# Graph attention: query and key products moved by one round, into the rounds that also aggregate

## The reference, cut to what matters

```python
for l in range(L):                                    # L = 2, H = 8, DH = 64
    q = ((x @ Wq[l].T + bq[l]) * scaling).reshape(n, H, DH)
    k = (x @ Wk[l].T).reshape(n, H, DH)
    v = (x @ Wv[l].T).reshape(n, H, DH)
    scores = jnp.einsum('ehd,ehd->eh', q[tgt], k[srcidx])
    m = jax.ops.segment_max(scores, tgt, num_segments=n)
    p = jnp.exp(scores - m[tgt])
    s = jax.ops.segment_sum(p, tgt, num_segments=n)
    w = p / (s[tgt] + 1e-16)
    agg = jax.ops.segment_sum(w[:, :, None] * v[srcidx], tgt, num_segments=n)
    attn = agg.reshape(n, D) @ Wo[l].T + bo[l]
    x = _batchnorm(x + attn, g1[l], beta1[l])
    ff = jax.nn.relu(x @ W1[l].T + b1[l]) @ W2[l].T + b2[l]
    x = _batchnorm(x + ff, g2[l], beta2[l])
```

## Time and profile before

| | |
|---|---|
| median of 3 runs | 1181.24 us |
| the profiled execution | 1181.42 us |
| its span in the trace | 1179.7 us |
| TensorE busy | 1076.4 us, 91% |
| VectorE busy | 642.7 us, 54% |
| ScalarE busy | 410.5 us, 35% |
| mean granted TensorE clock | 0.973 |
| attention of layer 0, rounds | about 505 to 738 us |
| attention of layer 1, rounds | about 835 to 1067 us |

### The profile page before, as it was taken

How to read it: one execution, slowest core, us unless ns; L and a number is a source line. 1 busy time by engine, 2 the same in 40 slices (tenths; PEclk the granted TensorE clock), 3 DMA queues, 4 the chain that set the end, 5 groups by cost and what they waited for, 6 DMA issues and landing times.

```text
span 1179.7 us, 14861 instructions
## 1 busy us (share of the span) xinstructions
PE 1076.4 (91%) x5638; PEld 693.6 (59%) x5638; DVE 642.7 (54%) x1162; ACT 410.5 (35%) x560; POOL 177.5 (15%) x119
## 2 busy tenths in 40 slices
PE   6999999899878999989999999989899999999914
PEld 2726446687657867656666666434566666664413
DVE  5685666446684145246565664541455555654495
ACT  2401112354323122045454554110455555551004
POOL 2000000997144420000000000000000000003000
PEclk9999999899989999999999999999999999999967
DMA  8001000002000310200000020110000000100002
GB/s 313 36 0 36 36 18 1 1 1 72 1 1 1 108 36 1 72 1 1 1 1 1 1 73 1 35 37 36 1 1 1 1 1 1 37 1 19 1 0 72
DMA packets 17659, 31.08 MB, mean 26 GB/s; under 512 B 3708, under 2 KB 4924, under 8 KB 17342
## 3 DMA queue, kind: packets, MB, share of 16 engines
q1 hardware_dynamic: 14270, 28.08, 6.8%
q10 hardware_dynamic: 3328, 2.15, 0.6%
HBM read 28.12 MB, written 2.10 MB: 26 GB/s over the span
## 4 chain that ended last, share of the span: by engine, by line
PE 81%; DVE 10%; ACT 3%; issue 2%; POOL 2%; DMA 1%; DVEq 0%; SPq 0%; ACTq 0%; POOLq 0%
PE slots L1516 71%; PE slots L1583 11%; DVE PT L1343 1%; DVE KS L1333 1%; DMA W<-in_wkT 1%; POOL KR L583 1%; ACT KS L873 1%; POOL MASK L584 1%; DVE rstd L1207 0%; DVE SM L1397 0%; DVE X L1409 0%; DVE XT L1291 0%; DVE P0L L1172 0%; DVE st L945 0%; DVE st L1414 0%
## 5 line engine op out<-in xcount | busy, mean ns | idle before, releaser
L1516 PE MATMUL slots<-XT,W 128*128 128x512 f32 x320 | 143.0, 599 | 0.0
L1516 PE MATMUL slots<-KS,QS 64*128 64x512 f32 x768 | 108.6, 416 | 18.3 <-DVE KS L1333 9.9
L1516 PE MATMUL slots<-PT,XN 128*64 128x256 f32 x1024 | 117.6, 382 | 0.0
L971 DVE COPY PT<-slots 128x1024 f32<-128x1024 f32 x64 | 78.2, 1222 | 71.1 <-PE slots L1583 70.1
L645 POOL TENSOR_TENSOR QS<-QF,QS 128x512 fp32r<-128x512 f32 x16 | 20.6, 1287 | 555.0 <-PE slots L1583 359.8
L1516 PEld LDWEIGHTS slots<-XT,W 128*128 128x128 f32 x320 | 59.1, 190 | 73.2 <-issue 71.5
L1516 PE MATMUL slots<-PT 128*128 128x512 bf16 (+3 forms) x408 | 96.9, 370 | 1.5 <-ACT PT L676 1.2
L1516 PEld LDWEIGHTS slots<-KS,QS 64*128 64x128 f32 x768 | 73.2, 190 | 39.9 <-issue 10.0
L1516 PEld LDWEIGHTS slots<-PT,XN 128*64 128x64 f32 x1024 | 70.7, 137 | 42.8 <-issue 9.8
L1343 DVE CUSTOM_DVE_ANT_0 PT<-slots,MASK 128x1024 f32<-128x1024 f32 x64 | 75.8, 1222 | 32.0 <-PE slots L1516 32.0
L1343 DVE CUSTOM_DVE_ANT_0 SM<-slots,MASK 128x1024 f32<-128x1024 f32 x64 | 75.8, 1222 | 30.5 <-PE slots L1516 30.5
(11 more groups left out here) (345 smaller groups left out, 1678.1 us busy)
## 6 DMA issues: line engine op xcount, KB each, us to landing
X<-in_x SPq DMA_DIRECT2D x4, 512.0 KB, 12.2
W<-in_wout SPq DMA_DIRECT2D x2, 1024.0 KB, 5.3
W<-in_gv SPq DMA_DIRECT2D x2, 1024.0 KB, 8.6
W<-in_gq SPq DMA_DIRECT2D x2, 1024.0 KB, 5.1
W<-in_gk SPq DMA_DIRECT2D x2, 1024.0 KB, 5.4
W<-in_go SPq DMA_DIRECT2D x2, 1024.0 KB, 6.6
W<-in_w SPq DMA_DIRECT2D x2, 1024.0 KB, 4.8
out<-X ACTq DMA_DIRECT2D x1, 1600.0 KB, 6.0
```

The lines of the kernel that those rows point to most:

```text
L971: nc.vector.tensor_copy(dst, src).then_inc(dve_evacuated, 1)
L1516: return nc.tensor.matmul(o_, lhsT, rhs, start=start, stop=stop)
```

## The change

Two conditions in `attention_order()` are moved by two units, that is by one round:

```diff
-        if n % 8 == 2 and 8 <= n < UNITS - 8:
+        if n % 8 == 4 and 8 <= n < UNITS - 8:
             order.append(("q", n // 8 + 1))
-        if n % 16 == 6 and n < UNITS - 16:
+        if n % 16 == 8 and n < UNITS - 16:
             order.append(("k", n // 16 + 1))
```

## The result

The changed kernel takes 1191.53 us, the median of 6 runs (1190.32 to 1198.02), against 1180.82 us for the kernel before on the same chip (1179.94 to 1181.65, 6 runs). The ratio is 1.0102 with a 95% interval of 1.0077 to 1.0126: slower by 1.0%, some 10.7 us between the medians. The profiled execution has a span of 1190.1 us, 10.4 more than before.

What follows compares the result with a forecast made beforehand. TensorE was taken to bound the kernel, its gaps set by score masking. Per layer 4.7 - 0.1 + 0.4 = 5.0 us, +9.9 for two, gave 1191.2 us; range 1187.8 to 1194.5.

Steps and rivals of the forecast that it cites:

- What bounds it: TensorE, busy 91% of the span; reordering acts only through its gaps, such as 0.62 us waiting for two score maskings.
- The number of waits: Per layer, TensorE waits on nm go from 5 to 12, on AG from 1 to 3, on KS from 4 to 1.
- Query products: Six moved per layer in front of an aggregation, leaving a bare round: +0.78 us each, +4.7 together.
- pair 10+12: Two rounds with a moved query product: 14.07 us before, 14.7 to 14.9 forecast, with a 0.6 us gap.
- Key products: Three moved per layer: the first saves 0.1 us, the other two cost +0.18 us each.
- Pair 6+8: Rounds of the first moved key product: its split's wait goes, round 6 becomes bare; -0.13 to -0.07 us, taken as -0.1.
- Pair 22+24: Rounds with reciprocal broadcast and a moved key product: from 19.20 to 19.35 to 19.41 us, taken as +0.18.
- The sum: One layer +5.0 us, bounds 3.8 and 5.3; two layers +9.9 us, 7.6 to 10.7.
- The prediction's lower limit of 1187.8: Total time: the terms' lower bound of 1189.0 us, widened by some 0.7 us for the spread of executions.
- What was moved along: Query scaling, rounding and split, and the later weight load: 0 us; exponentials keep a 0.3 us margin.
- The clock: Through the rounds' gaps TensorE's granted clock should stay at 1.00, the 2.4 GHz level.
- the rival of 1214 us: More frequent small gaps make TensorE's clock fall, 1.3 us lost at each, +23 us in all; chance 2%.

Runs made afterwards that it cites:

- run 4: Changed kernel plus repeated transposes of the odd unit after seven new bare rounds per layer: 4 of 8 repeated, 1191.54 us; all 8, 1194.16 us.
- run 7: Kernel before with key products in two half steps and first key ahead of second query, 1170.62 us; with layer 0's start reordered again, 1169.40 us.
- runs 6 and 7: First of these: kernel before with each layer's first key product moved ahead of its second query product, 1179.35 us; the other also splits key products into halves.

## Why the prediction was right

The forecast was 1191.2 us and the measured median is 1191.53. The mechanism was right, and the total is closer than its parts. Step by step:

- *What bounds it.* TensorE's gaps, and in them the masking. Shown: equal busy time, gaps that take 0.43 us of foreign work for nothing (run 4), and three more covers that save 4.5 to 4.8 us in a layer where 4.6 was said (run 7).
- *The number of waits.* 12, 3 and 1 were forecast, with 7.6, 2.7 and 2.5 us; the trace has 12, 3 and 1 with 7.7, 2.7 and 2.5.
- *Query products.* Forecast +0.78 each with bounds 0.61 and 0.83, measured +0.86 where the query stands directly in front of the aggregation (14.93 - 14.07, pair 10+12), a little outside. Both terms were a shade small: the query takes 3.63 us there (543.70 to 547.33) and not 3.60, and the turns to scores 2.63 us and not 2.58. In the rounds with rsum between them the query takes 3.54 as before (569.89 to 573.43), and the pair is +0.78. The six add 5.0 us to layer 0, 4.7 was said.
- *Key products.* Pair 6+8 has 19.00 us for 19.06, -0.06 for a forecast of -0.1. Pair 22+24 has 19.46 for 19.20, +0.26 for +0.18: the key product takes 7.06 us in front of the aggregation (586.03 to 593.09), where 6.97 to 7.03 was said, and the rest of the pair 12.40 for 12.38.
- *The sum.* 5.0 us a layer were forecast, with bounds of 3.8 and 5.3, and 5.45 were measured in layer 0 between first turns and projection, above the upper bound. In the traces the starts of the two layers took 1.6 us off again (1.27 and 0.31), since the changed kernel happened to run them at full clock, and the part ahead of the attention added 1.5. That the total came within 0.4 us is in part this cancelling, which was luck; the mechanism doesn't rest on it. The prediction's lower limit of 1187.8 also lies 0.5 us below what its terms give (1189.0 less 0.7), which changed nothing.
- *What was moved along.* The query's scaling, rounding and split, the later weight load and the exponentials cost nothing, as said: no new wait of turns on ACT appears in the rounds, and from projection to the next layer's scores it is 99.4 us in both.
- *The clock.* It stayed at 1.00 in all pairs of the table above, and from first turns to projection in both layers, so the rival of 1214 us falls. By a rule of the Trainium skill ("TensorE: Matmul & The Clock Gate", section "A second HAM failure mode: psum-queue depth-cycling"), brief and frequent idling between matmul groups can make the clock swing. In the rounds of the two kernels it is not borne out: gaps of 0.6 to 0.9 us left the clock alone, most of them one in 11 to 19 us and the first two in the changed kernel 4 us apart (ahead of the scores at 519.60 and 523.74), and filling them gave nothing back (run 4). At the end of a layer, where two waits of 0.68 and 0.89 us stand within 3 us, the clock did fall in 2 of 20 places (run 7), so small gaps are not harmless everywhere.

## What to carry to other kernels

Where PSUM slots go round in a fixed order, look at what stands between the filling of a slot and the next wait for it to be empty. A matmul group that needs no evacuated slot soon is worth most as the only work in such a place, and nothing beside work that is long enough already; count the bare places before and after, and price each with a row of the trace that has one. Before such a group is pulled forward, look also at what had covered its own operands: here a weight load came to light that cost 2.2 us where the wait that was removed had been 2.5.

## What was not expected of the hardware

The same wait has two outcomes for the clock. Ahead of the first scores TensorE stands still for 2.53 us in both kernels, after a long run of dense matmuls. Granted clock (the third number from the right) before, and then after:

```profile
505.00:508.50 3.50, 1.07 (x6) 0.96 (x8) 1.22 (x1) 0.96 (x1) 0.00 (x0) 0.85 0.00 0
508.50:512.00 3.50, 3.50 (x22) 2.69 (x18) 1.64 (x3) 0.37 (x1) 0.00 (x0) 0.67 0.00 0
```

```profile
505.00:508.50 3.50, 1.40 (x4) 0.33 (x2) 0.94 (x1) 1.02 (x1) 0.00 (x0) 1.00 0.00 0
508.50:512.00 3.50, 3.01 (x24) 2.50 (x24) 1.69 (x4) 0.14 (x1) 0.00 (x0) 1.00 0.00 0
```

In the one the clock was at the lower level for a part of the stretch, and 24 matmuls took 4.59 us; in the other they took 3.01 at full clock. Nine traces, with two layers each, have the same code and this wait at this place. In nine of the 18 places the 24 matmuls took 3.00 to 3.02 us, in the other nine 4.22 to 4.61, and from first scores to first turns it was then 4.31 to 5.59 us instead of 4.3, up to 1.3 us more. In runs 6 and 7 this wait is gone, and in their six places (two layers, three traces) the matmuls took 3.0 to 3.3 us. Differences of this kind between single executions say nothing about an edit. The first scores of layer 0 began between 506.9 and 510.3 us in those traced executions in which nothing ahead of them was changed; that such stretches after the long waits of the early part account for this is likely, but not shown. The mean granted clock of 0 to 506 us fits it: it was 0.97 in the two traces that came latest (510.2 and 510.3) and 0.98 in the others.
